# First stage of a four-layer sequence kernel: both batches kept on chip and interleaved, the stencil along time as a matmul

## The reference

```
x = x + L0(x)   # scores = tanh(x W1 + b1) v; softmax over the allowed l for every j; p @ x / count
                # mask by batch: l <= j, l >= j, or l != j
x = x + L1(x)   # zX*(neighbours in channel - 2y) + zY*(neighbours in time - 2y) + zR*y*(1-y), reflected edges
x = x + L2(x)   # bottleneck adapter chosen per batch, residual, layer norm
x = x + L3(x)   # three causal scans over time, gates, 512x512 products, layer norm
```

## Time and profile before

| | us |
|---|---|
| median of 3 runs (lowest, highest) | 844.01 (842.96, 844.47) |
| the profiled execution, whole time | 843.36 |
| its span, first to last instruction | 841.5 |
| PE busy in the span | 741.3 |
| DVE busy in the span | 616.2 |
| end of the first stage's last stencil | 243.3 |
| L1138 of group 0 starts | 288.5 |
| L739, an addition of 128x512 on DVE beside POOL, in the bias rows | 4.0 |

### The profile page before, as it was taken

The page is one execution under the profiler, slowest core; times in us unless marked ns, Lnnn a source line. Parts: engine busy times, 40 slices in busy tenths (PEclk is TensorE's granted clock), DMA queues, the critical chain, the costliest instruction groups (busy, mean ns, idle before and its releaser), DMA issues.

```text
span 841.5 us, 8347 instructions
## 1 busy us (share of the span) xinstructions
PE 741.3 (88%) x2916; PEld 528.6 (63%) x2916; DVE 616.2 (73%) x794; ACT 329.9 (39%) x686; POOL 197.4 (23%) x200
## 2 busy tenths in 40 slices
PE   4759767896606899999999999999999999999996
PEld 1424323443203686886877778688787777868775
DVE  4797987859862497588669759758866965975774
ACT  1223110321103434635633653563573365256234
POOL 4875572025722002102100210210110021021001
PEclk9869998899958899999999999999999999999999
DMA  7922556424265021113022021101202302110001
GB/s 235 328 100 63 150 182 235 182 63 136 94 198 144 1 34 16 45 57 50 1 101 50 1 100 32 19 34 67 51 0 100 51 1 100 28 24 23 28 1 50
DMA packets 36016, 66.86 MB, mean 79 GB/s; under 512 B 6758, under 2 KB 8390, under 8 KB 34962
## 3 DMA queue, kind: packets, MB, share of 16 engines
q1 hardware_dynamic: 26762, 52.47, 18.4%
q0 software_dynamic: 5728, 13.90, 7.9%
q10 hardware_dynamic: 3488, 0.01, 0.2%
HBM read 41.20 MB, written 16.78 MB: 69 GB/s over the span
## 4 chain that ended last, share of the span: by engine, by line
PE 63%; issue 14%; POOL 9%; DVE 5%; DMA 5%; ACT 2%; SPq 1%; POOLq 0%; DVEq 0%; ACTq 0%
PE bank L1052 17%; PE bank L1054 17%; PE bank L1053 17%; PE bank L1101 3%; PE bank L1086 3%; PE bank L1076 2%; POOL s_row L478 2%; DMA xb<-in_wg 2%; PE bank L1138 2%; PE bank L1108 2%; DMA xr<-rows_scratch 1%; DMA xr<-x_scratch 1%; POOL xt L484 1%; POOL xt L478 1%; DVE tr L1423 1%
## 5 line engine op out<-in xcount | busy, mean ns | idle before, releaser
L1052 PE MATMUL bank<-xh,wg_l 128*128 128x512 f32 x256 | 103.0, 402 | 0.0
L1054 PE MATMUL bank<-xh,wg_h 128*128 128x512 f32 x256 | 99.8, 390 | 0.0
L1053 PE MATMUL bank<-xl,wg_h 128*128 128x512 f32 x256 | 99.6, 389 | 0.0
L1347 POOL DMA_DIRECT2D xr<-rows_scratch x8 | 10.5, 1316 | 207.1 <-PE bank L1076 207.1
L1423 DVE TENSOR_TENSOR_SCAN tr<-alpha,carry,tr 128x512 f32<-128x512 f32 x48 | 58.9, 1269 | 0.0
L1053 PEld LDWEIGHTS bank<-xl,wg_h 128*128 128x128 f32 x256 | 48.1, 188 | 11.7 <-issue 1.9
L1052 PEld LDWEIGHTS bank<-xh,wg_l 128*128 128x128 f32 x256 | 48.1, 188 | 11.6 <-issue 1.9
L1052 PE MATMUL bank<-th,wt_l 128*128 128x512 f32 x128 | 52.9, 413 | 2.1 <-DVE tl L1435 2.1
L1054 PEld LDWEIGHTS bank<-xh,wg_h 128*128 128x128 f32 x256 | 48.1, 188 | 10.1
L1052 PE MATMUL bank<-xh,ws_l 128*128 128x512 f32 x128 | 53.4, 417 | 0.0
L1052 PE MATMUL bank<-wo_h,pl 128*128 128x512 f32 x128 | 50.6, 395 | 0.8 <-DVE pl L1445 0.8
(11 more groups left out here) (233 smaller groups left out, 1756.7 us busy)
## 6 DMA issues: line engine op xcount, KB each, us to landing
xb<-in_x SPq DMA_DIRECT2D x8, 1024.0 KB, 9.9
x_scratch<-xr SPq DMA_DIRECT2D x8, 1024.0 KB, 4.9
xr<-x_scratch SPq DMA_DIRECT2D x8, 1024.0 KB, 5.5
xr<-rows_scratch POOLq DMA_DIRECT2D x8, 1024.0 KB, 9.9
result<-xr SPq DMA_DIRECT2D x7, 1024.0 KB, 4.3
xt<-in_xT SPq DMA_DIRECT2D x6, 1024.0 KB, 8.5
xt<-xb SPq DMA_DIRECT2D x4, 896.0 KB, 5.4
dnb<-in_xT SPq DMA_DIRECT2D x2, 1024.0 KB, 12.5
```

What stands on the lines that cost most here:

```text
L1052: pe.matmul(acc, wl, xh_, start=start, stop=False)
L1053: pe.matmul(acc, wh, xl_, start=False, stop=False)
L1054: return pe.matmul(acc, wh, xh_, start=False, stop=stop)
```

## The change

The first stage is written anew, without loops: the two batches are both in `xb`, and every engine's stream holds batch 0 and batch 1 interleaved by hand. The scores of batch 1 are computed between the groups of batch 0. The time stencil is, for all 32 chunks, one float32 matmul with a tri-diagonal matrix `time_m` (zY beside the diagonal, the middle coefficient on it) and one one-pass matmul with `edge_sel` that adds the two neighbour rows of other chunks. SP gathers these rows for a group into `edge` (rows of 2 KB), ACT and DVE split them into `edge_hl`. The block sums put four chunks on four strips of 32 columns of the array and are folded by one more matmul (`replicate`). ACT squares `xb` in place of the pointwise part. POOL only makes constants. The split of `wg` and `wn1` moves to ACT and DVE late in the first stage; that of `wsoma`, `wtemp` and `wout` to ACT and DVE at the head of the second.

```diff
-                            last = pe.matmul(bank[5][:], wsel[:, c], xb[:, c], start=(c == 0),
-                                             stop=(c == NT - 1))
+                                last = pe.matmul(bank[G4[b]][Q * i:Q * i + Q], wsel[:, Q * c:Q * c + Q],
+                                                 xb[:, b, c], start=(j == 0), stop=(j == NG - 1),
+                                                 tile_position=(0, Q * i), skip_group_check=True)
...
-                                pe.matmul(acc, shift_m, xb[:, c], start=True, stop=False)
-                                pe.matmul(acc, last_m, xb[:, c - 1], start=False, stop=False)
-                                if c < NT - 1:
-                                    last = pe.matmul(acc, next_m, xb[:, c + 1], start=False, stop=True)
+            POOLED = [(3, 4), (1, 2, 4, 0)]
+            TIME = [(5, 7), (5, 7, 3, 6)]
...
+                        pe.wait_ge(x1_done, NT * b + c + 1)
+                        acc = bank[banks[c % len(banks)]][:]
+                        pe.matmul(acc, time_m[:, b], xb[:, b, c], start=True, stop=False)
+                        pe.wait_ge(edge_lo, NG * b + c // GT + 1)
+                        pe.matmul(acc, edge_sel[:, c % GT], edge_hl[:, (c // GT) % 2], start=False, stop=True)\
+                          .then_inc(time_mm, 1)
...
+                        act.wait_ge(edge_in[b][j], 16 * (3 if j in (0, NG - 1) else 2))
+                        act.activation(edge_hl[0:64, j % 2], edge[0:64], ACT.Copy, scale=coef[0:64, ZY, b:b + 1])\
+                           .then_inc(edge_hi, 1)
...
-                            po.tensor_tensor(dbuf[j], dbuf[j], xb[:, GT * j:GT * j + GT], ALU.mult)\
-                              .then_inc(d_mul, 1)
-                            po.tensor_tensor(before[j % 2], before[j % 2], after[j % 2], ALU.add)\
-                              .then_inc(nbr_sum, 1)
...
+                    def mix(b, j):
+                        banks = TIME[b]
+                        ve.wait_ge(sq_act, NG * b + j + 1)
+                        for i in range(GT):
+                            c = GT * j + i
+                            ve.wait_ge(time_mm, NT * b + c + 1)
+                            ve.scalar_tensor_tensor(sqb[:, j % 2, i], sqb[:, j % 2, i], coef[:, NEG_ZR, b:b + 1],
+                                                    bank[banks[c % len(banks)]][:], ALU.mult, ALU.add)\
+                              .then_inc(mixed, 1)
...
+                relu(0)
+                weight_hi(0, ws_h[:], pieces[0][0])
...
+                weight_hi(1, wt_h[:], pieces[1][0])
+                for t, k in halves:
+                    weight_hi(2, wo_h[:, k:k + 2], t[:])
                 for g in range(GROUPS):
...
+                weight_lo(2, wt_h[:], wt_l[:], pieces[1][0])
+                for i, (t, k) in enumerate(halves):
+                    weight_lo(3 + i, wo_h[:, k:k + 2], wo_l[:, k:k + 2], t[:])
```

More of the change, by code:

```diff
@@ L177, in build_program @@
[L177 to L188, removed]
@@ L375, in _ @@
[L375 to L390 removed]
+                    sp.wait_ge(hid_mm, 1)
@@ L571, in _, with hidden @@
+                    act.activation(wn1_h[:], stage_n1, ACT.Copy).then_inc(w_hi, 1)
+                    for j in range(NG):
+                        squares(1, j)
+                        edge_high(1, j)
                 @block.tensor
                 def _(pe):
+                    def hidden(b, j):
+                        n = NG * b + j
+                        pe.wait_ge(xt_in[b][j], 16)
+                        if b == 0 and j >= 2:
+                            pe.wait_ge(hid_act, j - 1)
+                        elif b == 1 and j == 0:
+                            pe.wait_ge(hid_act, NG)
+                        elif b == 1:
+                            pe.wait_ge(hid_act, n)
+                        for k in range(KE):
+                            last = pe.matmul(bank[HID[b][j]][:], w1_sb[:, k], xt_slot[b][j][:, k],
+                                             start=(k == 0), stop=(k == KE - 1))
+                        last.then_inc(hid_mm, 1)
@@ new lines, in _ @@
+                    hidden(0, 0)
+                    hidden(0, 1)
+                    scores(0, 0)
+                    hidden(0, 2)
+                    scores(0, 1)
+                    hidden(0, 3)
+                    scores(0, 2)
+                    scores(0, 3)
+                    block_sums(0)
+                    weight_sums(0)
+                    hidden(1, 0)
+                    replicate(0)
+                    block_transposes(0)
+                    prob_transposes(0)
+                    hidden(1, 1)
@@ new lines, in _ @@
+                    for c in range(0, 9):
+                        pooled(0, c)
+                    scores(1, 0)
+                    for c in range(0, 4):
+                        time_part(0, c)
+                    for c in range(9, 13):
+                        pooled(0, c)
+                    scores(1, 1)
+                    hidden(1, 2)
+                    for c in range(4, 8):
+                        time_part(0, c)
+                    for c in range(13, NT):
+                        pooled(0, c)
@@ new lines, in _ @@
+                    hidden(1, 3)
+                    for c in range(8, 12):
+                        time_part(0, c)
+                    scores(1, 2)
+                    scores(1, 3)
+                    block_sums(1)
+                    weight_sums(1)
+                    for c in range(12, NT):
+                        time_part(0, c)
+                    replicate(1)
+                    block_transposes(1)
+                    prob_transposes(1)
+                    for c in range(0, 9):
+                        pooled(1, c)
@@ new lines, in _ @@
+                    for j in range(NG):
+                        read_scores(0, j)
+                    softmax_in(0)
+                    block_low(0)
+                    params_a()
+                    normalise(0)
+                    sums_low(0)
+                    rows()
+                    for c in range(0, 5):
+                        x1(0, c)
+                    channel_part(0, 0)
+                    for c in range(5, 9):
+                        x1(0, c)
+                    edge_low(0, 0)
@@ new lines, in _ @@
+                    mix(0, 0)
+                    stencil(0, 0)
+                    read_scores(1, 0)
+                    channel_part(0, 1)
+                    for c in range(9, 13):
+                        x1(0, c)
+                    edge_low(0, 1)
+                    mix(0, 1)
+                    stencil(0, 1)
+                    read_scores(1, 1)
+                    channel_part(0, 2)
+                    for c in range(13, NT):
+                        x1(0, c)
+                    edge_low(0, 2)
@@ new lines, in _ @@
+                    mix(0, 2)
+                    stencil(0, 2)
+                    read_scores(1, 2)
+                    read_scores(1, 3)
+                    softmax_in(1)
+                    channel_part(0, 3)
+                    edge_low(0, 3)
+                    block_low(1)
+                    mix(0, 3)
+                    stencil(0, 3)
+                    normalise(1)
+                    sums_low(1)
+                    params_b()
+                    for c in range(0, 5):
+                        x1(1, c)
@@ new lines, in _ @@
+                    channel_part(1, 0)
+                    for c in range(5, 9):
+                        x1(1, c)
+                    edge_low(1, 0)
+                    mix(1, 0)
+                    stencil(1, 0)
+                    weight_low(0, wg_h[:, 0:KE], wg_l[:, 0:KE], stage_g[:, 0:KE])
+                    channel_part(1, 1)
+                    for c in range(9, 13):
+                        x1(1, c)
+                    edge_low(1, 1)
+                    mix(1, 1)
+                    stencil(1, 1)
@@ new lines, in _ @@
+                    weight_low(1, wg_h[:, KE:], wg_l[:, KE:], stage_g[:, KE:])
+                    channel_part(1, 2)
+                    for c in range(13, NT):
+                        x1(1, c)
+                    edge_low(1, 2)
+                    mix(1, 2)
+                    stencil(1, 2)
+                    weight_low(2, wn1_h[:], wn1_l[:], stage_n1)
+                    channel_part(1, 3)
+                    edge_low(1, 3)
+                    mix(1, 3)
+                    stencil(1, 3)
@@ L1014, in build_program @@
         o_out = sem("o_out")
+        w2_in = [sem(f"w2_in{i}") for i in range(3)]
+        w2_hi = sem("w2_hi")
+        w2_lo = sem("w2_lo")
         rows2_in = sem("rows2_in")
```

1156 lines of the change are left out of this document (578 added, 578 removed).

## The result

The changed kernel takes 830.37 us (median of 3 runs, 828.41 to 830.98), the kernel before 844.01 in the same series (3 runs, 842.96 to 844.47). The ratio is 0.9835, 95% interval 0.9806 to 0.9865: faster by 1.6%, and 27 us slower than the 803 of the prediction, outside its range of 788 to 824.

A forecast was written before the change was run, and what follows sets the result against it. DVE was taken to pace the first stage's stencil stretches and PE the unchanged second stage. Start 51.0, work 109.5, waits 28.2 and clock 11 gave 199.7, 43.6 earlier; with hand-over +2.5, 803 us, range 788 to 824.

The forecast's parts named there:

- Up to the first x1, 51.0: Start of the first stage: batch 0's first x1 comes at 51.0 us, 23.3 earlier than before.
- DVE's work, 109.5: From the first x1 to the last stencil, DVE's own instructions sum to 109.5 us, with POOL silent.
- DVE's waits, 28.2: In the same stretch, DVE waits 28.2 us in all, mostly at `mix` for PE's `time_part`.
- 4.4 and 2.4 us ahead of `mix` of groups 1 and 2: Batch 0: PE's scores and `hidden` of batch 1 delay `mix`, 4.4 us for group 1 and 2.4 for group 2.
- PE's clock ... 5 x 2.2: 11; bounds 0 and 20: First stage: after five PE waits of 5 to 7 us the clock halves, costing `mix` 2.2 us each, 11 in all.
- T: End of the first stage's last stencil: 243.3 us before, predicted at 199.7, 43.6 earlier.
- `pooled` starts 1.09 us apart: First stage on PE: two `pooled` chunks start 1.09 us apart, so five x1 per batch wait 0.4 us each.
- Hand-over +2.5: Last stencil to the second stage's L1138: 45.2 us plus 2.5, for 2 MB of weights travelling beside the bias row.
- strips in series: Rival: the block sums' four strips run one after the other, 14.3 us more, 817 us; chance 0.25.
- edge rows waited for: Rival: edge rows land late behind loads and stores in SP's queue, 3 us per group, 827 us; chance 0.07.
- Fewer waits: Rival: PE keeps its clock in the first stage, 11 us less, 792 us; chance 0.13.
- PE never gets the full clock in the first stage: Rival: about 90 us of PE's first-stage work run at half clock, 882 us, slower than before; chance 0.03.

The follow-up runs named there:

- experiment 3: On top of the changed kernel with 96 rows, each block sum uses all 128 columns instead of a strip of 32: 824.45 us, +14.5 against 96 rows alone.
- order: On top of the changed kernel with 96 rows, PE's batch 0 list reordered so `hidden` and scores fill gaps in `pooled`: 800.80 us, -9.1 against 96 rows alone.
- warm: Changed kernel with its 48 rows, PE's 3.5 us wait ahead of batch 1's `pooled` filled with four unused products: 818.67 us, 11.7 us less.
- late_w: On top of the changed kernel with 96 rows, `wtemp` and `wout` loaded only after group 0's bias row landed: 806.28 us, -3.7 against 96 rows alone.

## Why the prediction was wrong

- **Up to the first x1, 51.0**: right, 50.51. The strips ran side by side: 3.4 us were predicted for the 16, and the chain has

```profile
33.62 3.57 PE bank L574 x32
```

  Their price if in series, +14.3, was measured as +14.5, the closeness being luck (experiment 3). The estimate of 4.5 us beside it is 4.3 by its own terms (16 x 0.86, divided by 2.38 x 4 / 3).
- **DVE's work, 109.5**: right within 3 us, 112.4. A whole-group instruction takes 2.27 to 2.35 us now that POOL is silent; the 6.48 of the earlier trace rows is gone.
- **DVE's waits, 28.2**: nearly right without the two faults below. With 96 rows and the clock kept they are 142.95 - 112.08 = 30.9. The 4.4 and 2.4 us ahead of `mix` of groups 1 and 2 are supported by order (-9.1), though that gain also holds some clock.
- **"PE's clock ... 5 x 2.2: 11; bounds 0 and 20"**: this is the step that failed. It measured 27.6 in the trace (T from 227.9 to 200.35) and 28.9 in the medians. It was counted from waits of 5 to 7 us alone, at 2.2 us each from the earlier trace rows. The five waits were there, 4.5 to 6.2 us long. But the 3.5 us wait ahead of batch 1's chunks lowered the clock too, and the loss behind it was not 2 but 12 us (by warm), since the clock stayed down for 27. A wait of 4.5 us ahead of `mix` of batch 0's last group, also not counted, cost 1.4. And the first of the five cost more than its price: PE starts again at 78.06 and is at half until 90.75, 6.4 us lost, though behind two chunks it runs products of 128 rows there:

  ```profile
  78.06:91.00 12.94, 12.94 (x21) 5.80 (x22) 2.85 (x4) 0.00 (x0) 0.00 (x0) 0.51 0.00 1
  ```

  The other four cost about 3 each. Half of PE's 66 busy us at half clock in this stage is 33 us; 27.6 of it was in DVE's way. A price per wait is only right where the clock comes back as fast as in the row that it is from.
- **`pooled` starts 1.09 us apart**: also failed, by 0.39 a chunk; 4.6 to 7.0 us in all. The products between the starts of the earlier trace rows have 96 rows (timeline of PE before), and the change makes them 48. I carried the duration over without comparing the shape.

  ```profile
  180.01 0.80 PE L644 MATMUL bank<-g_hl,bw_hl 96*128 96x512 f32 x1
  ```

- The account, by the profiled ends of the first stages (good to about 3 us each, so the small terms only say that nothing large is missing): clock 27.6 - 11 = 16.6, rows 7.0, DVE's other waits 30.9 - 28.2 = 2.7, work 112.1 - 109.5 = 2.6, the start -0.6: 28.3, of the 28.2 that T is late (227.9 for 199.7).
- **Hand-over +2.5**: right, 47.7 - 45.2 = 2.5, but as the sum of two terms. The bias row's load takes 14.89 us for 10.58, 4.3 more, and late_w shows that the 2 MB beside it are the cause. Against that the load of x2 starts 1.25 us ahead of the last stencil's end instead of 0.3 behind it, and takes 8.52 for 9.07 us: 2.1 less, where the prediction had "the same distance". The price was too small, and the number came right by the other.
- **Second stage unchanged**: right.
- **Rivals**: strips in series and edge rows waited for are both refuted by runs, and no wait of DVE for ACT's squares shows. "Fewer waits" (792) had the direction of the clock wrong. "PE never gets the full clock in the first stage" (882, chance 0.03) named the mechanism that acted, in part: the clock stood at half for 78 us, and of PE's work 27.6 us (counted at the full clock) ran at half in DVE's way, against the 52 from which it would have made the kernel slower.

## What to carry to other kernels

When a product shrinks to 64 rows or fewer beside products of 128 (between 64 and 96 nothing was tried), price the two switches around it (0.39 us here), pad its operands with zeros to 96 rows, or group the small ones; compare the shape of the row a duration comes from with the new shape. Where another engine sets the pace and TensorE waits a few us at a time, walk its list for each wait and for what runs behind it, since products whose result is dropped can be cheaper than the clock that a wait costs. First try to move real work into the gap, as `order` does.

## What the runs showed of the hardware

- A float32 product of 128 rows and a one-pass product of 48 or 64: 1.48 us a chunk at the full clock, 2.70 to 2.73 at half (48 rows); with 96 rows 1.09.
- After a wait of 3.5 us TensorE stayed at 1.2 GHz for 27 us while busy throughout (48 rows), for about 7 us (64 rows, or 48 with half the switches) and for under 4 us (96 rows).
- 41 useless products, 20 us more of PE's time, made the kernel 13 us faster.
- A 1 MB accumulating load landed in 9.8 us, and in 14.3 with 2 MB of plain loads issued just ahead of it.
- Sixteen float32 products on four strips of 32 columns take 3.57 us, against 13.98 at the full width: 3.9 times. TensorE: Matmul & The Clock Gate in the Trainium skill, section "Part 3: Packing small matmuls — row/col tiling", reports 2.38 for three strips; the trace has close to the number of strips for four.
